# Spectra of a Fourier layer stored as (ky, kx, image) in place of image by image

## The reference, cut to what matters

```
M1, M2, WIDTH, LAYERS = (16, 16, 64, 4)
def _spectral_conv(h, w1, w2):
    xf = jnp.fft.rfft2(h)
    top = jnp.einsum('bixy,ioxy->boxy', xf[:, :, :M1, :M2], w1)
    bot = jnp.einsum('bixy,ioxy->boxy', xf[:, :, -M1:, :M2], w2)
    of = jnp.zeros(xf.shape, dtype=xf.dtype)
    of = of.at[:, :, :M1, :M2].set(top)
    of = of.at[:, :, -M1:, :M2].set(bot)
    return jnp.fft.irfft2(of, s=(h.shape[-2], h.shape[-1]))
h = jnp.einsum('bhwi,ic->bhwc', x, fc0_w) + fc0_b
h = h.transpose(0, 3, 1, 2)
for l in range(LAYERS):
    sc = _spectral_conv(h, w1r[l] + 1j * w1i[l], w2r[l] + 1j * w2i[l])
    pw = jnp.einsum('bihw,oi->bohw', h, pw_w[l]) + pw_b[l][None, :, None, None]
    y = sc + pw
    ...  # batch norm over (image, pixel), affine
    h = jax.nn.gelu(y, approximate=False)
```

## Time and profile before

| | us |
|---|---|
| median of three runs | 2528.74 |
| the profiled execution, whole | 2528.25 |
| its span, first to last instruction | 2526.5 |
| PE busy (matmul) | 2173.5 (86%) |
| ACT busy | 1669.2 (66%) |
| DVE busy | 1648.5 (65%) |

### The profile page before, as it was taken

The page is one execution under the profiler, slowest core; times in us unless marked ns, Lnnn a source line. Parts: engine busy times, 40 slices in busy tenths (PEclk is TensorE's granted clock), DMA queues, the critical chain, the costliest instruction groups (busy, mean ns, idle before and its releaser), DMA issues. The chain is left out here.

```text
span 2526.5 us, 79368 instructions
## 1 busy us (share of the span) xinstructions
PE 2173.5 (86%) x34571; PEld 1449.5 (57%) x34571; DVE 1648.5 (65%) x2562; ACT 1669.2 (66%) x2640; POOL 152.0 (6%) x172
## 2 busy tenths in 40 slices
PE   6769979976997998599979967995999599964999
PEld 4657757765665776566657765664222355552444
DVE  3868878874777887577778874775000677754444
ACT  1924468876776887777778885675999466641333
POOL 0000000000000000000000000000000022202443
PEclk9989989988998999899989988998999699976999
DMA  5655567758997774899977659997652100012433
GB/s 184 227 169 203 185 255 260 240 177 274 343 349 283 265 262 151 276 329 331 323 269 257 217 201 302 360 370 274 218 178 88 37 2 2 2 29 55 105 87 71
DMA packets 174006, 518.62 MB, mean 205 GB/s; under 512 B 22687, under 2 KB 37759, under 8 KB 173439
## 3 DMA queue, kind: packets, MB, share of 16 engines
q1 hardware_dynamic: 173663, 513.55, 60.6%
HBM read 343.73 MB, written 170.37 MB: 203 GB/s over the span
## 5 line engine op out<-in xcount | busy, mean ns | idle before, releaser
L426 PE MATMUL P<-cst,mem 128*128 128x128 f32 (+1 forms) x3760 | 500.9, 282 | 54.2 <-DMA mem<-in_x 14.5
L426 PEld LDWEIGHTS P<-cst,mem 128*128 128x128 f32 (+1 forms) x3760 | 414.7, 143 | 162.2 <-issue 129.8
L685 ACT ACTIVATE mem<-P,small 128x512 f32<-128x512 f32 x512 | 310.6, 688 | 287.3 <-PE P L534 263.6
L844 DVE BATCH_NORM_STATS2 mem<-mem 128x6 f32<-128x512 f32 x512 | 315.2, 678 | 4.8 <-ACT mem L685 4.8
L882 DVE COPY mem<-P 128x512 f32<-128x512 f32 x384 | 247.9, 687 | 99.6 <-PE P L426 98.5
L534 PEld LDWEIGHTS P<-cst,mem 64*128 64x128 f32 (+1 forms) x5120 | 240.5, 166 | 100.7 <-issue 100.3
L534 PE MATMUL P<-cst,mem 64*128 64x128 f32 (+1 forms) x5120 | 262.6, 275 | 3.8 <-issue 3.5
L675 ACT ACTIVATE mem<-mem,small 128x1024 f32<-128x1024 f32 x192 | 229.2, 1250 | 49.7 <-DMA mem<-z_d 49.6
L837 DVE COPY mem<-P 128x512 f32<-128x512 f32 x256 | 165.0, 686 | 123.2 <-PE P L511 123.2
L832 DVE COPY mem<-P 128x512 f32<-128x512 f32 x256 | 165.3, 687 | 112.9 <-PE P L426 112.9
L719 ACT ACTIVATE mem<-mem,small 128x1024 f32<-128x1024 f32 x192 | 232.3, 1249 | 1.0
(11 more groups left out here) (164 smaller groups left out, 2941.1 us busy)
## 6 DMA issues: line engine op xcount, KB each, us to landing
mem<-z_d SPq DMA_DIRECT2D x348, 512.0 KB, 5.2
z_d<-mem SPq DMA_DIRECT2D x256, 512.0 KB, 6.2
mem<-in_wmix SPq DMA_DIRECT2D x64, 1024.0 KB, 8.6
G_d<-mem SPq DMA_DIRECT2D x128, 256.0 KB, 4.0
mem<-G_d SPq DMA_DIRECT2D x128, 256.0 KB, 7.6
hz<-z_d SPq DMA_DIRECT2D x64, 512.0 KB, 4.6
mdB<-dT_d SPq DMA_DIRECT2D x44, 384.0 KB, 5.6
mem<-in_x SPq DMA_DIRECT2D x128, 12.0 KB
```

The source lines that it names most:

```text
L426: return nc.tensor.matmul(out, in_, ident[0:n, 0:n], start=True, stop=True, is_transpose=True)
L685: nc.scalar.activation(ychunk(l, a, h), P[4 + 2 * (a.q % 2) + h][:, :], ACT.Identity, bias=bias0 if first else pwb_c).then_inc(S["eY"], 1)
L844: nc.vector.bn_stats(so, ychunk(l, a, h)).then_inc(S["eS"], 1)
```

## The change

`XX` is laid out as (ky, kx, image): image has a step of 1 float, kx of 32, ky of 512. The gathers of a step then read 1024 consecutive floats. The copies that fill `XX` write the same numbers from the same PSUM places as before, but with ky innermost, so with a step of 512 floats (2048 bytes) between consecutive writes. The one small addition on the 32 zero-frequency terms in layer 0 now works on 32 consecutive floats. The number and the size of all instructions, the waits and the transfers stay as they are.

```diff
         def spectra(s):
-            return XX.rearrange("p (i k y) -> p y k i", k=16, y=KY)[:, 2 * s:2 * s + 2]
+            return XX[:, s * 1024:s * 1024 + 1024].rearrange("p (n i) -> p n i", i=IMG)
+
+        def image_modes(rows, image):
+            return XX.rearrange("p (y k i) -> p i k y", y=KY, k=16)[rows, image]
 
         def operands(s):
-            return SG[s % 3].rearrange("p (b k v i) -> p v b k i", b=2, k=16, v=2)
+            return SG[s % 3].rearrange("p (n v i) -> p v n i", v=2, i=IMG)
 
         def spectrum(r, image, q):
-            o = image * MODES + q * 256
-            return XX[r * 64:r * 64 + 64, o:o + 256].rearrange("p (i n) -> p i n", i=4)
+            return image_modes(slice(r * 64, r * 64 + 64), image)[:, q * 8:q * 8 + 8].rearrange("p (i j) y -> p i j y", j=2)
 
         def spectrum_bank(h, r):
-            return P[7][h * 64:h * 64 + 64, :].rearrange("p (i r n) -> p r i n", i=4, r=2)[:, r]
+            return P[7][h * 64:h * 64 + 64, :].rearrange("p (i r j y) -> p r i j y", i=4, r=2, j=2)[:, r]
...
-                    last = nc.scalar.activation(XX[0:64, m:m + MODES], P[2 * (b % 2)][o, :], ACT.Copy)
+                    last = nc.scalar.activation(image_modes(slice(0, 64), h * PAIRS + b), P[2 * (b % 2)][o, :].rearrange("p (k y) -> p k y", k=16), ACT.Copy)
...
-                    last = nc.vector.tensor_scalar(XX[64:128, m:m + MODES], P[2 * (b % 2) + 1][o, :], -1.0, None, ALU.mult)
+                    last = nc.vector.tensor_scalar(image_modes(slice(64, 128), h * PAIRS + b), P[2 * (b % 2) + 1][o, :].rearrange("p (k y) -> p k y", k=16), -1.0, None, ALU.mult)
...
-            dc = XX[0:64, :].rearrange("p (i m) -> p i m", m=MODES)[:, :, 0]
+            dc = XX[0:64, 0:IMG]
```

More of the change, by code:

```diff
@@ L640, in _ @@
                 for h in range(2):
-                    o, m = slice(h * 64, h * 64 + 64), (h * PAIRS + b) * MODES
-                    last = nc.scalar.activation(XX[0:64, m:m + MODES], P[2 * (b % 2)][o, :], ACT.Copy)
+                    o = slice(h * 64, h * 64 + 64)
+                    last = nc.scalar.activation(image_modes(slice(0, 64), h * PAIRS + b), P[2 * (b % 2)][o, :].rearrange("p (k y) -> p k y", k=16), ACT.Copy)
                 last.then_inc(S["a0_re"], 1)
```

## The result

| | before | after |
|---|---|---|
| median of the runs | 2526.13 us (6 runs, 2523.18 to 2538.08) | 2545.61 us (6 runs, 2536.91 to 2550.84) |
| profiled execution | 2528.25 us | 2542.83 us |
| its span, granted clock | 2526.5 us, 0.937 | 2541.0 us, 0.935 |

The ratio is 1.0053, with an interval from 1.0028 to 1.0078. The forecast was 2522 us for the profiled execution; it took 2542.83.

The account below looks back on a forecast made before the run. It took ACT to bound the products and PE the steady forward transform. From 2528.25 us, 37 of gain and 31 of loss gave 2522, no measurable change; the range holding 8 in 10 was 2502 to 2550.

Parts of the forecast that it names:

- Layer 0: Copies filling layer 0's spectra: strided writes make ACT the bound, 34.2 us in place of 28, a loss of 6 us.
- ACT's free step in the products: Products: without store waits, ACT's step falls from 3.25 us to 2.17, or 2.2 with PE late next.
- rival 1: Products: stores don't hold ACT, so each phase gains 13 us, 52 in all, giving 2507; chance 0.17.
- rival 2: Forward transform: strided writes at 2048 bytes cost more, DVE and ACT become the bound, giving 2561, slower; chance 0.18.
- it waits 3 to 3.5 us, and afterwards the DMA (1.75 a step) keeps up: Products: ACT's step 8 copies wait for step 4's stores, then no more, leaving 10 us gain a phase in layers 1 to 3.
- The term of 37 us of gain: Products, four phases: cheaper gathers less waits for stores gain 10 us in each of layers 1 to 3, 7 in layer 0.
- Its own sentence on what would prove it wrong: Wrong if floats written 2048 bytes apart cost otherwise than at 188, or store time depends on neighbours otherwise than by issue order.
- The second term: Forward transforms of layers 1 to 3: strided spectrum copies lose 12.6 us in the steady part and 12 at the ends.
- 42 x 0.3: Steady forward part: some 14 pairs in each of three layers lose 0.3 us each, 12.6 us in all.
- PE's wait: Steady forward part: PE waits for DVE's longer spectrum copies and loses 0.25 us a pair.
- ACT's part: Steady forward part: ACT's longer copies cost next to nothing given about 2 us idle a pair; 0.05 us added.
- at the ends: End of each forward transform: three DVE and two ACT copy groups stand in the chain, 4.1 us a layer, 12 in all.

Follow-up runs that it names:

- e4: The changed kernel with the four late weight transfers (steps 12 to 15) cut to a sixteenth, 64 KB each: 2525.05 us, ratio 1.0008 to the kernel before.
- e8: e7 with parameters loaded before step 0 and late weights issued behind the stores of steps 2, 4, 6, 8 instead of 0 to 3: 2517.05 us, ratio 0.996.
- e7: The changed kernel with each half of a pair's spectrum copied by DVE and ACT, two copies each instead of four by one: 2522.75 us, ratio 0.999.

## Why the prediction was wrong, step by step

**Right.** All prices of single instructions: the gather 1054 ns (1060 forecast), L898 605 (about 600), L748 619 (617), L815 694 and L814 690 (under 1000), L644 1036 (1069). Layer 0: +5.4 (+6), with ACT as its bound. ACT's free step in the products: 2.19 us (2.17 to 2.2). That stores hold ACT at all, against rival 1, and that a store of the middle of the phase releases L664. What rival 2 lived on, a dearer price per float at 2048 bytes, did not happen.

**The step that failed: "it waits 3 to 3.5 us, and afterwards the DMA (1.75 a step) keeps up".** The term of 37 us of gain came to 22.7. It treated the stores as a line behind the weights in the order of issue, each at full rate, from which one wait at step 8 follows. What happened is 8.8 to 9.9 us of waits a phase, in layer 1 five of over 1.5 us, beginning at step 5. The part of the term that was wrong is the full rate from the first issue on. By the prediction's own figures the stores of step 1 land 13.2 us after the phase's start (5.6 + 1.75 + 2.6 + 1.75 + 1.5); they landed 18.2 after it, and those of step 4 29.6 after it in place of 26. The order of landing was nearly that of issue. But in its first 9 us this mixture of stores and loads moved 208 GB/s in place of the 305 to 410 of the sum (window, length, busy us PE, PEld, DVE, ACT, POOL, clock, DMA share, GB/s):

```profile
549.00:558.00 9.00, 7.63 (x261) 7.49 (x259) 5.04 (x8) 8.28 (x12) 0.00 (x0) 1.00 0.80 208
```

The kernel before moved 194 GB/s in the like stretch of its own phase (538.9 to 547.9); the forecast's rates came from a later stretch. Afterwards the stores of each step landed 3.8 us behind those of the last, at the full rate, and that is the pace of steps 5 to 8 (3.75 to 3.95 us). Why the rate is low at first was not tried. The 1.5 us to land is an estimate that no run shows by itself. So a store lands 9 us after its issue in place of 3.5 (e4), and a ring of four buffers allows it only four steps: 13 us at the old pace, 8.8 at the new one. The prediction quoted the right number, stores that took "7 to 9" at the slow pace, as a point against rival 1, and did not set it against 4 x 2.19. Its own sentence on what would prove it wrong, a store's time that depends on what runs beside it in another way than the order of issue, comes close to what occurred: the order held, the rate did not.

**Left out altogether:** SP's eight parameter loads. They occupy SP for 7.8 us in the middle of the phase, and stores of finished steps queue behind them. Before, the pace was slow enough to hide that; DMA work then falls away just when it is wanted. The windows of the kernel after, before and within those loads (columns as above):

```profile
562.00:565.00 3.00, 1.91 (x64) 1.91 (x66) 1.38 (x2) 1.19 (x3) 0.00 (x0) 1.00 1.03 412
...
574.00:577.00 3.00, 2.25 (x78) 2.11 (x75) 1.53 (x3) 2.93 (x5) 0.00 (x0) 1.00 0.23 45
```

The DMA engines go from full to a quarter. Nor do these waits account for the phase by subtraction: layer 1's 52.3 less 8.8 would be 43.5, but with the stores nearly out of the way (e8, 1.2 us of waits) it takes 48.7, as ACT then waits 7.7 us for PE. PE's pauses are in no term of the prediction.

**The second term: forward +24.6, measured +32.6.** Steady part: "42 x 0.3" was 36 intervals between DVE's copies (12 a layer) that grew by 0.62 each, which would be 22.3. Measured are 4.7, 7.5 and 6.3 us by layer, 18.5 in place of 12.6, because some pairs of before were longer than 10.81 already (layer 1 has four of 11.31 to 12.32) and absorbed part of it. Of the 0.62, PE's wait of 0.24 was forecast (0.25), but not that a run of 16 transposes cut in two takes 0.2 more beside the wait (1.53 + 0.63 in place of 1.97); and ACT's part was 0.19, not 0.05. The rest, +14.1 against +12, is at the ends, in layer 1 5.1 us where 4.1 were summed; that excess is wider than the copies' added time and was not taken apart.

**The sum.** 14.3 of gain missing and 8.0 more loss, less 0.6 in layer 0 and 0.6 in all else, is 21 us: 2522 becomes 2543, and the profiled execution took 2542.83. The range held the time only because it reached to the milder half of rival 2. The sign came out as in that rival, but by another mechanism: the price per float stayed at the forecast level, and the time came from the products' gain falling short and from smaller losses of overlap.

## What to carry to other kernels

When a change makes a stage faster, hold each buffer ring of that stage against the new pace: ring depth times the new step must exceed the landing time of the transfer that frees the buffer, taken from the busiest stretch of the trace and not from its bytes over bandwidth. Slack of an engine counts only at the instruction that is made longer; sum what stands behind that instruction up to the next one that PE waits for. And compare layouts with their surroundings fitted: here the change lost 19 us as made, and with its queues put in order it was some 6 us ahead of the old layout in the same surroundings, which were fitted to the new one alone. Last, look again after each limit is lifted: behind the waits for stores stood PE's own pauses, and from e7 to e8 ACT's waits for stores fell by 20.1 us while those for PE grew by 14.8.

## What the runs showed of the hardware that was not expected

- A strided fp32 write from PSUM costs next to nothing at two floats to 16 bytes (30 ns of 592 on ACT, none on DVE) or in runs of two, about half of the price at step 3, 0.95 ns a float on ACT and 0.73 on DVE from step 4 on, and much more at 24 floats alone (1440 and 1434 ns where 16 and 31 have 1013 to 1088). Why 24 stands out was not tried.
- The gathers on DVE read 1024 consecutive floats in 690 to 694 ns, half of the 1382 with a step, and less per float (0.68 ns) than any copy from PSUM here (512 in 690). The Trainium skill (VectorE: DVE Perf Modes, What auto-detection actually checks) has a mode of twice the rate for one source and a destination both in SBUF, and asks no step of one of them. By that rule alone the strided gather would have been as fast; the trace shows it half as fast, and the measurement decides. No run here tells whether the mode was off there or its gain lost on the reads.
- 256 KB stores land 3.5 us after issue (median) with 64 KB loads between them and 9 (up to 11.5) with 1 MB loads in flight from the same queue; the loads themselves take 9.7 to 11.8.
- PE's runs of small matmuls in the products break mostly after 126 to 128 of them, for 0.3 to 3.8 us in the kernel after, and go on 2.2 to 2.8 us after a 16 KB packet of the instruction queue has started. In the phases of products these pauses sum to 36 us, and to about half with the small weights (e4).
